# Where the rows of a later step and a weight matrix are loaded: one DMA behind each block, and behind the one-hots instead of ahead of them

## What is computed

```python
def cell(h, x):                       # a GRU cell, 64 steps in time, 64 rows, 512 columns
    gi = x @ W_ih + b_ih
    gh = h @ W_hh + b_hh
    i_r, i_z, i_n = jnp.split(gi, 3, axis=-1)
    h_r, h_z, h_n = jnp.split(gh, 3, axis=-1)
    r = jax.nn.sigmoid(i_r + h_r)
    z = jax.nn.sigmoid(i_z + h_z)
    n = jnp.tanh(i_n + r * h_n)
    return (1.0 - z) * n + z * h
...
x = x + ffn_fp8(scan(cell, cond, x))  # a feed-forward layer, its inputs and weights rounded to fp8
```

## Time and profile before

| | us |
|---|---|
| Median of 3 runs | 2875.74 (2875.29 to 2877.38) |
| Span of the profiled execution | 2879.2 |
| PE busy in that span | 2562.9 (89%) |
| DVE, ACT, POOL busy | 1685.2, 1140.6, 1262.3 |
| x product of step 2 (stage 2) | 688.1 to 783.8 |
| x product of step 3 (stage 4) | 1336.1 to 1428.4 |

### The profile page before, as it was taken

The page is one execution under the profiler, slowest core; times in us unless marked ns, Lnnn a source line. Parts: engine busy times, 40 slices in busy tenths (PEclk is TensorE's granted clock), DMA queues, the critical chain, the costliest instruction groups (busy, mean ns, idle before and its releaser), DMA issues. The chain is left out here.

```text
span 2879.2 us, 154632 instructions
## 1 busy us (share of the span) xinstructions
PE 2562.9 (89%) x67605; PEld 1681.0 (58%) x67605; DVE 1685.2 (59%) x3398; ACT 1140.6 (40%) x2317; POOL 1262.3 (44%) x598
## 2 busy tenths in 40 slices
PE   2088999998889999999999999999996999999995
PEld 1066777776768888887675564655642444444442
DVE  8852222225632222225646778867592888888887
ACT  1321222225632222224702333323232777777773
POOL 0255666662046666664061363622700333333334
PEclk8599999999999999999999999999998999999998
DMA  6833222224422222226554253442432223232322
GB/s 193 239 85 77 74 73 71 73 71 112 131 63 71 74 73 70 73 71 167 152 135 127 92 151 118 115 156 85 129 143 93 74 84 95 84 95 84 95 63 53
DMA packets 234843, 293.74 MB, mean 102 GB/s; under 512 B 69581, under 2 KB 194023, under 8 KB 233895
## 3 DMA queue, kind: packets, MB, share of 16 engines
q1 hardware_dynamic: 212743, 240.84, 30.6%
q10 hardware_dynamic: 18304, 36.19, 3.6%
q0 software_dynamic: 3680, 15.21, 1.9%
HBM read 231.61 MB, written 60.45 MB: 101 GB/s over the span
## 5 line engine op out<-in xcount | busy, mean ns | idle before, releaser
L1145 PE MATMUL psum<-second_shared 64*32 64x384 f16 x32768 | 1026.0, 324 | 50.2 <-issue 31.3
L1153 PE MATMUL psum<-low_w,low_hot 64*32 64x384 f16 x16384 | 756.5, 324 | 2.0 <-issue 2.0
L1372 DVE TENSOR_SCALAR second_shared<-psum 32x384 f16<-32x384 f32 x496 | 272.3, 549 | 749.1 <-PE psum L1145 741.9
L953 POOL TENSOR_TENSOR low_hot<-first_shared,sum_mask 128x1024 f16<-128x1024 f16 x256 | 499.8, 1952 | 430.1 <-DVE first_shared L1359 183.8
L1145 PEld LDWEIGHTS psum<-second_shared 64*32 64x32 f16 x32768 | 561.5, 93 | 198.0 <-issue 89.8
L947 POOL TENSOR_TENSOR second_shared<-first_shared,whole_mask 128x2048 f16<-128x2048 f16 x128 | 462.5, 3614 | 460.1 <-PE psum L1145 348.2
L1044 ACT ACTIVATE second_shared<-psum 32x384 f16<-32x384 f32 x496 | 239.8, 483 | 801.9 <-PE psum L1145 795.9
L1233 PE MATMUL psum<-low_w,low_hot 64*64 64x384 f16 x12288 | 513.7, 326 | 19.9 <-issue 13.5
L1233 PEld LDWEIGHTS psum<-low_w,low_hot 64*64 64x64 f16 x12288 | 378.3, 108 | 150.4 <-issue 18.4
L310 PE MATMUL psum<-w_x,x_cols 128*64 128x512 f32 (+1 forms) x1856 | 312.0, 495 | 9.5 <-ACT x_cols L280 9.5
L1153 PEld LDWEIGHTS psum<-low_w,low_hot 64*32 64x32 f16 x16384 | 282.5, 93 | 56.8 <-issue 3.1
(11 more groups left out here) (286 smaller groups left out, 2746.6 us busy)
## 6 DMA issues: line engine op xcount, KB each, us to landing
low_w<-w_rows SPq DMA_DIRECT2D x384, 144.0 KB
low_w<-w_rows SPq DMA_DIRECT2D x256, 120.0 KB
second_shared<-w_rows SPq DMA_DIRECT2D x1024, 24.0 KB, 1.9
x_gates<-x_out ACTq DMA_DIRECT2D x58, 384.0 KB, 2.3
xg<-x_gates SPq DMA_DIRECT2D x58, 384.0 KB, 3.2
low_w<-w_rows SPq DMA_DIRECT2D x256, 72.0 KB
low_w<-w_rows SPq DMA_DIRECT2D x384, 48.0 KB
w_rows<-quantised SPq DMA_DIRECT2D x24, 384.0 KB, 4.9
```

The source lines that it names most:

```text
L953: nc.gpsimd.tensor_tensor(low_hot[:, buf].rearrange("p (s k) b -> p s k b", s=SUBS), low_a[:, slot, bass.ds(c, 1), :, :].rearrange("p a s ...
L1145: last = nc.tensor.matmul(run[m][u][j * Q:(j + 1) * Q, :], whole_hot[rows[u], m, sign, kk, j % 2 * Q:(j % 2 + 1) * Q], whole_w[rows[u], m, ...
L1153: nc.tensor.matmul(run[m][u][j * Q:(j + 1) * Q, :], low_hot[rows[u], m, kk, j % 2 * Q:(j % 2 + 1) * Q], low_w[rows[u], m, at:at + UC], sta ...
L1372: last = nc.vector.tensor_scalar(whole_w[u * B:u * B + Q, m, 0, bq, :], run[m][u][bq * Q:(bq + 1) * Q, :], 1.0 / HIGH_ONE, None, ALU.mult)
```

## The change

Two orders are changed, and no instruction of a computing engine is added or removed. On SP, the x rows of step 1 are no longer loaded in two bursts: from block 4 of step 2's x product on, one of their 24 DMAs stands behind the weights of each block, so that the last one stands behind block 27. SP waits ahead of the first of them for the one-hots of step 0, as before. The 32 blocks are now written out, where before the last 16 were a loop. On ACT, the one-hots of step 3 come first and the four DMAs of `w_x` behind them; the wait for PE's last pair block is gone.

```diff
-            def load_low(eng, operand, kinds, slot):
+            def low_rows(eng, operand, kinds, slot):
 
                 for r, kind in enumerate(kinds):
                     for u in range(2):
                         at = u * B + r * SK
                         eng.dma_start(low_a[at:at + SK, slot].rearrange("k c s b -> k (c s) b"),
                                       pieces[operand, kind]).then_inc(rows_of_in[slot], 16)
-
-            def load_whole(eng, operand, m, slot):
+                        yield
+
+            def whole_rows(eng, operand, m, slot):
...
+                            yield
+
+            def low_then_whole(eng, operand, m, slot):
+
+                yield from low_rows(eng, operand, LOW_ROWS, slot)
+                yield from whole_rows(eng, operand, m, slot)
...
-                        for c in range(4 * BUFS):
+                        next_rows = low_then_whole(sp, 1, 0, ROWS_X0)
+                        for c in range(NBK):
                             load(2, 0, c, sum_buf(c))
-                            if c == 2 * BUFS - 1:
+                            if c == BUFS:
                                 sp.wait_ge(hot_ok, block_no(2, 0, 0) + 1)
-                                load_low(sp, 1, LOW_ROWS, ROWS_X0)
-                        load_whole(sp, 1, 0, ROWS_X0)
-                        sum_blocks(sp, sum_load(2, 0), 4 * BUFS, 4 * BUFS)
+                            if c >= BUFS:
+                                next(next_rows, None)
...
                         bases(1)
-                        a.wait_ge(run_ok[1], block_no(3, 0, 0) + BUFS)
+                        x_one_hots(3)
                         for k in range(KD):
                             a.dma_start(w_x[:, k, :], w_ih[k * P:(k + 1) * P, :]).then_inc(w_x_in, 16)
-                        x_one_hots(3)
```

More of the change, by code:

```diff
@@ L257, in load_whole, with load_low @@
                                           pieces[operand, kind].rearrange("k (c s) b -> s k c b", s=SUBS)[sub]).then_inc(rows_of_in[slot], 16)
+                            yield
+            def low_then_whole(eng, operand, m, slot):
+                yield from low_rows(eng, operand, LOW_ROWS, slot)
+                yield from whole_rows(eng, operand, m, slot)
+            def load_low(eng, operand, kinds, slot):
+                for _ in low_rows(eng, operand, kinds, slot):
+                    pass
+            def load_whole(eng, operand, m, slot):
+                for _ in whole_rows(eng, operand, m, slot):
+                    pass
             def x_banks(rows, *gates):
```

## The result

The changed kernel takes 2859.44 us, the median of four runs (2854.61 to 2865.69), against 2876.56 us of the kernel before in the same comparison (four runs, 2875.29 to 2879.65). That is 17.1 us less; the ratio is 0.9934 with a 95% interval of 0.9914 to 0.9954. The forecast was 2855.7 us, 20.0 less. The profiled execution of the changed kernel took 2854.61 us and has a span of 2852.8 us.

A forecast was written before the change was run, and what follows sets the result against it. PE bounds the kernel, standing still in stages 2 and 4 for weights behind row loads and for late one-hots. Gains of 12.0 and 8.0 us make 20.0 off 2875.7, so 2855.7 us, range 2852.5 to 2862.5.

The forecast's parts named there:

- the 18 to 22 us that had a chance of 0.72: Whole kernel: nearly all of the forecast gain of 20.0 us arrives; chance 0.72.
- a late start of step 2's sum: Start of step 2's sum: PE waits because of the moved plain x weights; up to 5 us in the range.
- a loss in stage 2: Stage 2, x product of step 2: 6 us of its 12.0 us gain stays out, giving 2861.7 us.
- The margin of 0.05 us: Stage 2: SP's issue with a 32 KB row load, 2.56 us, stays below PE's 2.61 us a block.
- the 0.44 us for each load: Stage 2: each row load in flight ahead delays a block's weights by 0.44 us.
- the 3.5 us of hidden lateness: Stage 2: about 3.5 us of lateness of a block's weights costs PE nothing.
- the 0.6 us taken off for blocks 3 and 4: Stage 4's start: 0.6 us off the 8.6 us gain for late weights beside POOL's gathers, leaving 8.0 us.
- the step that failed: Stage 4's end: plain x weights issued after ACT's last one-hots, about 1411.7; cost nothing, up to 5 us in the range.
- The first: Start of step 2's sum: plain x weights make PE wait 2 to 5 us, 2858 to 2861 us; chance 0.13.
- The second rival: Stage 2: single row loads hold up weights by over 3.5 us, losing 6 us, 2861.7 us; chance 0.08.
- the third: Whole change does nothing: weights wait on something other than row loads, stops only move; 2870 to 2876 us; chance 0.04.
- the last: Stage 2: SP becomes the bound; at 3.7 us a block the time is 2881.8 us; chance 0.03.

The follow-up runs named there:

- group of eight: Changed kernel with its 24 row loads in three groups of eight, behind blocks 4, 12 and 20: 2871.74 us, ratio 0.9975 to the kernel before.
- groups of eight and of four: The fours: changed kernel with its row loads in six groups of four, behind blocks 4, 8, ..., 24: 2864.13 us, ratio 0.9949 to the kernel before.

## Why the prediction was right, and where not

**Faster, and by how much: right.** The time lies in the range and its sign was forecast. The gain is 17.1 us where 20.0 were forecast, and less than the 18 to 22 us that had a chance of 0.72. The range holds it because it left room for a late start of step 2's sum and for a loss in stage 2; neither came, and something else cost about as much. That much is luck. The profiles account for 15.7 (stage 2: 12.1, stage 4: 3.6), 16.5 and 16.2 us in the three profiled executions of the changed kernel, and the medians of its three comparisons for 17.1, 15.6 and 15.4. The two profiled spans first compared differ by 26.4 us; some 10 of that lie in stages that the change does not touch and come from the two executions, not from the change. The time of the profiled execution after is 1.8 us above its span (2854.61 and 2852.8). If the same holds before, that one took about 2881.0 us, 5.3 above its median of 2875.74, while the one after lies 4.8 below its own.

**Stage 2: right in its size and its reasons.** The 12.0 us are there (83.5 us, and 83.4 to 84.9 in the other profiles with this order). SP's issue for a block and its row load was put at 2.19 and 2.56 us; 1.73 + 0.33 = 2.06 and, from row to row, 2.65 were measured. The margin of 0.05 us is thus not there: behind the 32 KB loads lateness does pile up, by 0.04 us a block, 0.3 in eight, which the buffers hide. The sum of SP's issues also left out single long ones, such as 1.50 us at 688.45, and these were hidden too. The second and third group of eight bear out the 0.44 us for each load and the 3.5 us of hidden lateness; at the start of the stage less is hidden, as the first groups of eight and of four show. Single loads cost short waits of 0.4 to 0.8 us in all in three of the eight profiles that have them, and none in the other five.

**Stage 4, its start: right.** The stop of 5.02 us, the slow blocks behind it and the later wait are gone. Of the 0.6 us taken off for blocks 3 and 4, 0.5 is there (10.69 us for four blocks of 2.61, and 0.26 us of wait), and it stands ahead of block 4 and is for weights, as the prediction had it. In the other profiles with this start the stage loses between nothing and 0.6 us there.

**Stage 4, its end: the step that failed.** It is the time of the issue of `w_x`. The prediction put it at the time when "ACT's last one-hots end", asked only what comes after ("now they share the DMA engines with SP's index loads and the first weights of step 2"), and took nothing for it beyond 5 us in the range. The prediction's time for the end of the one-hots, some three blocks before PE's end, was right: 1394.93, 7.8 us before 1402.7. But the issue came 2.1 us before that, while SP was issuing the weights of block 31, the last that PE needs in the stage, which the step had left out. At the time that it named, "nothing" would have been right: the kernel that waits for the one-hots is that case, and its stage takes 83.39 us. With the issue where it really came the runs show a stop of 2.4 to 2.9 us in every profile with this order of ACT's list and no later wait, with the last block at up to 4.5 us in place of 2.61 behind it: 2.8 to 4.7 us in all, the part of the gain that is missing. Taking `w_x` away from that moment in three ways (behind PE's end, behind ACT's one-hots, into step 1) brought stage 4 to 83.4 to 83.6 us each time. With the first of them both stages give 12.2 + 8.8 = 21.0 us in the profile, and the medians 19.7 and 18.2: the gain that was forecast for the change.

**The rivals.** The first, that the plain x weights hold up the start of step 2's sum, named the right load and gave a time that fits (2858 to 2861), but at the wrong place: the sum starts without a wait in every profile, even with `w_x` issued 2 to 10 us later. The wait came at the end of the stage before. No rival named block 31's weights, since the working looked at one victim only, and the fit of this rival's time is chance. The Trainium skill (DMA: Bandwidth & Descriptors, section "Queues, rings and completion order") has a DMA engine take turns between queues packet by packet. Packets of 5.5 KB (3.15 MB in 576) on ACT's queue against 1.4 KB (4.33 MB in 3064) on SP's are why a small load can be late behind a large one by that rule, if the profile's packets are taken for the page's. The trace agrees: the two queues moved 324 and 379 packets from 1395 to 1403 us, and 413 and 409 from 1340 to 1350 us in the kernel before, where `w_x` stood beside the first weights of stage 4. The order of single packets on one engine is not shown. The second rival (half of stage 2 lost) needed eights, not ones; the third and the last found no support in any profile.

## What to carry to other kernels

A load that is needed later should be spread one by one behind loads that are needed now: what it may cost can be read from how late the queue already is and how much of that the buffers hide; in this kernel less was hidden at the start of the stage. When a large load is moved to where "nobody waits for it", look at the other queue's last issues before that moment, not only the ones after it: their data is still on the way. And a DMA issue that stands behind computing instructions on the same engine does not thereby come after them; if it is to, give it a semaphore to wait for. And where a row names what ended a wait, look when that was done: in two of the rows here the named one-hots had been there for microseconds, and the wait was for a load.

## What was not expected of the hardware

- ACT's queue issued a DMA without a wait when only two of the last block's eight activations, which stand ahead of it in the list, had begun: 2.1 us early (1392.84 against 1394.93). With a wait on their semaphore it came behind them, and this alone removed a stop of about 2.7 us. The Trainium skill (PSUM — Partial Sum Buffer, section "Engine vs sequencer instructions") keeps the instructions of an engine's datapath apart from those that its sequencer carries out; of a nop it says that the sequencer waits only until the instructions ahead of it are dispatched, not until they are complete. The trace shows a DMA issue behave so. So a list is not worked off in order throughout, as the section on the chip has it: six of those activations began after the issue that stands behind them.
- The same stop left PE's next block at 4.31, 2.79 and 4.26 us in three executions of one kernel; the stretch of the first has a granted clock of 0.63, between the levels of 1.2 and 2.4 GHz as a mean, behind a stand of under 3 us, and that of the second 1.00. In the kernel with groups of eight a stand of 3.45 us left the next eight blocks at 20.99 us, the full pace: in these profiles the length of a stand does not tell what clock follows it.
- Stages that nothing touched differ between executions by as much as the smaller terms that were argued about: the pair blocks of step 0 begin at 148.82 and end at 687.67 in the profile before, and run from 147.10 to 683.86 in the one after, 538.9 against 536.8 us; over all profiles they take up to 540.5. A single pair of spans would have shown 26.4 us for a change that is worth about 16.
- In every profile one or two of SP's issues between 688 and 702 us take 0.97 to 1.75 us, where most take 0.3 to 0.45 (in the changed kernel 1.50 at 688.45 and 1.21 at 695.30). Beside each the trace has a packet of 16 KB on a queue of the kind `instruction`, and the issue ends about 0.4 us after that packet has ended. Not every such packet has a long issue beside it, and that the one holds up the other is not tested.
